# The activation turned by VectorE and through DRAM with a later down projection, and taps' operands of 64 rows for two heads side by side

## The reference

```python
# L0, a long convolution along each sequence, for 32 channels h and 64 batches
mask = (jnp.arange(Lq) < length[:, None]).astype(u.dtype)
u_m = u * mask[:, None, :]
kernel = _get_kernel(log_dt, C, log_A_real, A_imag, Lq)      # 32 x 512 taps
y = irfft(rfft(u_m, 2 * Lq) * rfft(kernel, 2 * Lq))[..., :Lq]
y = (y + u_m * D[:, None]) * mask[:, None, :]
x = x + y
# L1, a gated projection with a low-rank term for each batch
gate = lora_add(x @ W_gate.T, x, A_gate, B_gate)             # 512 -> 1376
up = lora_add(x @ W_up.T, x, A_up, B_up)
act = jax.nn.silu(gate) * up
out = x + lora_add(act @ W_down.T, act, A_down, B_down)      # 1376 -> 512
```

## Time and profile before

| | us |
|---|---|
| median of 3 runs | 544.09 |
| lowest, highest | 543.97, 545.04 |
| profiled execution | 544.7 |
| its span | 543.0 |
| TensorE busy | 505.7 |
| VectorE busy | 344.3 |
| ScalarE busy | 190.5 |
| one tile of the loop | 28.56 |

### The profile page before, as it was taken

How to read it: one execution, slowest core, us unless ns; L and a number is a source line. 1 busy time by engine, 2 the same in 40 slices (tenths; PEclk the granted TensorE clock), 3 DMA queues, 4 the chain that set the end, 5 groups by cost and what they waited for, 6 DMA issues and landing times.

```text
span 543.0 us, 10229 instructions
## 1 busy us (share of the span) xinstructions
PE 505.7 (93%) x3045; PEld 459.8 (85%) x3045; DVE 344.3 (63%) x812; ACT 190.5 (35%) x411; POOL 41.5 (8%) x55
## 2 busy tenths in 40 slices
PE   0098889999999999999999999999999999999997
PEld 0097787989898999989898989898989898999986
DVE  7883266757483939383848475766758483939381
ACT  6790007433333333232324232333333333324220
POOL 1006700101000000000000001000001000001000
PEclk9999899999999999999999999999999999999999
DMA  7899993424132323232323323131414132424200
GB/s 278 277 365 388 320 332 68 111 56 111 46 111 48 114 52 114 52 108 57 96 64 95 66 80 82 53 96 49 114 49 109 43 110 52 114 52 114 53 19 21
DMA packets 68403, 61.59 MB, mean 113 GB/s; under 512 B 41634, under 2 KB 50242, under 8 KB 68386
## 3 DMA queue, kind: packets, MB, share of 16 engines
q1 hardware_dynamic: 68386, 61.39, 39.4%
HBM read 52.89 MB, written 8.47 MB: 113 GB/s over the span
## 4 chain that ended last, share of the span: by engine, by line
PE 86%; DVE 6%; DMA 5%; ACT 1%; issue 1%; SPq 0%; DVEq 0%
PE ps_g L1024 21%; PE ps_u L1024 21%; PE ps_db L1062 13%; PE ps_da L1062 13%; PE ps_x L1004 3%; PE ps_g L978 3%; DMA toep<-kpad 2%; PE ps_x L1053 2%; DMA kpad<-k_sb 2%; PE ps_u L978 2%; PE ps_u L1035 2%; PE ps_u L1034 2%; PE ps_g L1034 2%; PE ps_g L1035 2%; PE ps_da L1123 1%
## 5 line engine op out<-in xcount | busy, mean ns | idle before, releaser
L494 ACT CAST b_spl<-b_raw 64x512 fp32r<-64x512 f32 (+1 forms) x96 | 54.7, 572 | 97.1 <-PE ps_u L1035 78.1
L870 DVE STREAM_TRANSPOSE ps_x<-h_act 32x128 f32<-32x128 f32 x240 | 77.4, 323 | 3.8
L1024 PE MATMUL ps_g<-w_hi,x_hi 128*128 128x512 f32 (+1 forms) x192 | 71.2, 371 | 1.4 <-DVE x_lo L935 1.4
L1024 PE MATMUL ps_u<-w_hi,x_lo 128*128 128x512 f32 (+1 forms) x192 | 71.5, 372 | 0.0
L1024 PE MATMUL ps_u<-w_hi,x_hi 128*128 128x512 f32 (+1 forms) x192 | 71.4, 372 | 0.0
L1024 PE MATMUL ps_u<-w_lo,x_hi 128*128 128x512 f32 (+1 forms) x192 | 71.3, 372 | 0.0
L1024 PE MATMUL ps_g<-w_hi,x_lo 128*128 128x512 f32 (+1 forms) x192 | 71.3, 371 | 0.0
L1024 PE MATMUL ps_g<-w_lo,x_hi 128*128 128x512 f32 (+1 forms) x192 | 71.2, 371 | 0.0
L822 DVE TENSOR_TENSOR b_spl<-b_raw,b_spl 64x512 fp32r<-64x512 f32 (+1 forms) x96 | 63.5, 662 | 4.4 <-ACT b_spl L494 0.7
L1062 PE MATMUL ps_da<-wd_hi,ht_hi 128*128 128x288 f32 (+1 forms) x176 | 54.6, 310 | 0.2 <-DVE ht_lo L879 0.2
L1062 PE MATMUL ps_db<-wd_hi,ht_hi 128*128 128x288 f32 (+1 forms) x176 | 53.1, 302 | 0.0
(11 more groups left out here) (166 smaller groups left out, 939.2 us busy)
## 6 DMA issues: line engine op xcount, KB each, us to landing
a_raw<-atab SPq DMA_DIRECT2D x64, 152.0 KB, 2.3
toep<-kpad SPq DMA_DIRECT2D x16, 512.0 KB, 7.4
b_raw<-btab SPq DMA_DIRECT2D x128, 64.0 KB, 2.1
um<-xr SPq DMA_DIRECT2D x16, 256.0 KB, 5.6
x<-xT SPq DMA_DIRECT2D x8, 512.0 KB, 6.6
w_raw<-wgu SPq DMA_DIRECT2D x8, 512.0 KB, 9.2
xrow<-x_sq SPq DMA_DIRECT2D x64, 64.0 KB, 2.2
y_sb<-xrow SPq DMA_DIRECT2D x16, 256.0 KB, 2.7
```

Source lines behind the costliest of these rows:

```text
L494: nc.scalar.copy(b_spl[0:LR, up, 0:w], b_raw[slot][:, up * w:(up + 1) * w]).then_inc(b_hi, 1)
L870: ins = V.transpose(into[:, :, tok * Q:(tok + 1) * Q], src[:, :, to * Q:(to + 1) * Q])
L1024: T.matmul(ps[:, 0:w], xs[:, kb, :], ws[:, kb, col:col + w], start=(kb == 0 and xs is x_hi and ws is w_hi), stop=False)
```

## The change

Two edits go together.

**Taps of 64 rows.** `toep` has 64 rows for each head of the pair, head 0 on partitions 0 to 63 and head 1 on 64 to 127, each with 576 taps; two DMAs load it. Since a block of 128 input positions is now two halves of 64, `conv` issues for each distance d and each half one matmul of 64 rows for head 0 and one for head 1, which write to the two banks of one PSUM pair. There are three such pairs (`ps_gg`, `ps_uu`, `ps_xx`, the last being the two banks `ps_x`). The host lays out `xr` accordingly.

**Turned activation.** In tiles 1 to 14 all three chunks, in tile 0 chunks 1 and 2, and in tile 15 chunk 0 go through DRAM: VectorE transposes squares of 32 x 32 into `h_sq` (chunks 0 and 2) or `x_sq` (chunk 1) (`square_h`), `store_h` writes them in four DMAs to `hrow`, `load_h` reads the turned rows to one of two buffers `h_raw`, and ScalarE and VectorE split them from there. The other chunks of tile 0 and tile 15 are turned by TensorE. The down projection of chunks 1 and 2 (`down_rest`) moves to the next tile's time, behind its chunk 0; `transpose_td`, `down_lora` and `finish` move behind it. `h_act` has one buffer instead of two. On the A and B rows: `b_raw` is one tensor whose two slots lie on different partitions, and `load_bd` and `load_b` change places.

The diff, cut to its core:

```diff
+RP = 3
+HR = P // 2
+HW = NL + HR
...
+        hrow = nc.dram_tensor("hrow", (FB * P, P), F32, kind="Internal")
...
-            toep = sb(pa, "toep", [P, RC, 2, NL])
+            toep = sb(pa, "toep", [P, RC, HW])
...
-        h_act = sb(top, "h_act", [P, 2, 512])
+        h_act = sb(top, "h_act", [P, 512])
...
+        h_sq = sb(top, "h_sq", [P, 512])
...
+        h_raw = [sb(top, f"h_raw{i}", [P, 4, P]) for i in range(2)]
...
-        ps_g = [top.enter_context(nc.psum_tensor(f"ps_g{i}", [P, 512], F32)) for i in range(2)]
-        ps_u = [top.enter_context(nc.psum_tensor(f"ps_u{i}", [P, 512], F32)) for i in range(2)]
+        ps_c = [top.enter_context(nc.psum_tensor(name, [P, 2, 512], F32)) for name in ("ps_gg", "ps_uu", "ps_xx")]
+        ps_g, ps_u, ps_x = ([both[:, i, :] for i in range(2)] for both in ps_c)
...
+        def shifted_taps(pair, h):
+
+            return bass.AP(tensor=kpad, offset=(2 * pair + h) * (P + NL) + 1, ap=[[1, HR], [1, HW]])
...
-                sp.dma_start(toep[:, slot, :, :], shifted_taps(pair)).then_inc(toep_in[slot], 16)
+                for h in range(2):
+                    sp.dma_start(toep[h * HR:(h + 1) * HR, slot, :], shifted_taps(pair, h)).then_inc(toep_in[slot], 16)
...
+            def store_h(t, c):
+                col, w = CH[c]
+                sp.wait_ge(hsq_ok, NC * t + c)
+                for part in range(P // Q):
+                    rows = x_sq if c == 1 else h_sq
+                    src = rows[part * Q:(part + 1) * Q, 0:w].rearrange("q (f t) -> q f t", t=Q)
+                    into = bass.AP(tensor=hrow, offset=col * P + part * Q, ap=[[P, Q], [Q * P, w // Q], [1, Q]])
+                    sp.dma_start(into, src).then_inc(h_out, 16)
+
+            def load_h(t, c):
+                f0, nf = BLK[c]
+                full = nf if c < NC - 1 else nf - 1
+                sp.wait_ge(h_out, 16 * (P // Q) * (NC * t + c))
+                src = bass.AP(tensor=hrow, offset=f0 * P * P, ap=[[P, P], [P * P, full], [1, P]])
+                sp.dma_start(h_raw[c % 2][:, 0:full, :], src).then_inc(h_in[c], 16)
+                if full < nf:
+                    sp.dma_start(h_raw[c % 2][0:FLAST, full, :],
+                                 hrow.ap()[(f0 + full) * P:(f0 + full) * P + FLAST, :]).then_inc(h_in[c], 16)
...
+                if not first:
+                    store_h(t, 0)
+                if not last:
                     load_b(na, nq, 0, ids)
+                if not first:
+                    load_h(t, 0)
+                if not last:
+                    load_a(na, nq, ids)
+                    store_h(t, 1)
                 if not first:
                     store(*((a, 0) if q == 1 else (a - 1, 1)))
                 if not last:
-                    load_a(na, nq, ids)
+                    load_h(t, 1)
+                    store_h(t, 2)
+                    load_b(na, nq, 1, ids)
+                    load_h(t, 2)
+                    store_x(t + 1)
                     load_bd(na, nq, ids)
-                    load_b(na, nq, 1, ids)
-                    store_x(t + 1)
                     load_y(t + 1, nq)
...
+                def square_h(c):
+                    n = NC * t + c
+                    dve.wait_ge(act_ok, n + 1)
+                    if c == 1:
+                        dve.wait_ge(xrow_out, 16 * (P // Q) * (t + 1))
+                    else:
+                        wait(dve, h_out, 16 * (P // Q) * (n - 1 - c // 2))
+                        wait(dve, htlo_ok, (NC + 1) * t + c // 2)
+                    V.transpose((x_sq if c == 1 else h_sq)[:, 0:CH[c][1]], h_act[:, 0:CH[c][1]]).then_inc(hsq_ok, 1)
...
+                wait(pe, x1_ok, pair - RP + 1)
+                if pair == RP - 1:
+                    pe.wait_ge(amaskt_ok, 1)
+                for d in range(KB):
+                    for half in range(2):
+                        at = d * P + (1 - half) * HR
+                        for h in range(2):
+                            rows = slice(h * HR, (h + 1) * HR)
+                            v = um[rows, slot, half * KB * NB:half * KB * NB + (KB - d) * NB]
+                            last = T.matmul(ps_c[pair % RP][:, h, d * NB:KB * NB], toep[rows, slot, at:at + P], v,
+                                            start=(d == 0 and half == 0), stop=(d == KB - 1 and half == 1))
                 last.then_inc(conv_ps, 1)
...
-                wait(pe, htlo_ok, (NC + 1) * (t - 1) + 1)
+                wait(pe, tm_ok, t)
...
+            def down_rest(t):
+                pe.wait_ge(htlo_ok, (NC + 1) * t + 2)
+                down_chunk(1)
+                pe.wait_ge(htlo_ok, (NC + 1) * (t + 1))
+                for f in range(BLK[2][0], FB):
+                    ins = down(f, 1)
+                ins.then_inc(ad_ps, 1)
+                for f in range(BLK[2][0], FB):
+                    ins = down(f, 0)
+                ins.then_inc(down_ps, 1)
...
                 base(0, 0)
-                if not first:
-                    transpose_td(t - 1)
                 if first:
                     lora_a(t)
-                    base(0, 1)
-                    lora(0, 0)
-                else:
-                    lora(0, 0)
-                    base(0, 1)
+                base(0, 1)
+                lora(0, 0)
                 lora(0, 1)
                 if not first:
-                    down_lora(t - 1)
-                for up in range(2):
-                    base(1, up)
-                    lora(1, up)
+                    down_rest(t - 1)
+                base(1, 0)
                 if first:
                     transpose_act(0)
-                for up in range(2):
-                    base(2, up)
-                    lora(2, up)
-                transpose_act(1)
-
-                pe.wait_ge(htlo_ok, (NC + 1) * t + 1)
+                else:
+                    transpose_td(t - 1)
+                lora(1, 0)
+                base(1, 1)
+                lora(1, 1)
+                if not first:
+                    down_lora(t - 1)
+                base(2, 0)
+                if last:
+                    transpose_act(1)
+                lora(2, 0)
+                base(2, 1)
+                lora(2, 1)
                 wait(pe, y_ok, 2 * t)
                 if first:
                     pe.wait_ge(w_rem_dve, len(pieces) - NP_POOL)
                 pe.wait_ge(ad_lo, t + 1)
+                pe.wait_ge(htlo_ok, (NC + 1) * t + 1)
                 down_chunk(0)
-                transpose_act(2)
-                pe.wait_ge(htlo_ok, (NC + 1) * t + 2)
-                down_chunk(1)
-                if not last:
+                if last:
+                    transpose_act(2)
+                    down_rest(t)
+                else:
                     lora_a(t + 1)
```

More of the change, by code:

```diff
@@ L178, in program @@
         g_ps, u_ps, silu_ok, act_ok = sem("g_ps"), sem("u_ps"), sem("silu_ok"), sem("act_ok")
[L179 removed]
+        hsq_ok, h_out, ht_ps, hthi_ok, htlo_ok = (sem("hsq_ok"), sem("h_out"), sem("ht_ps"), sem("hthi_ok"),
+                                                  sem("htlo_ok"))
+        h_in = [sem(f"h_in{c}") for c in range(NC)]
         ad_ps = sem("ad_ps")
@@ L886, in body @@
+                gated(0)
+                if not first:
+                    square_h(0)
+                b_lo_part(a, q, 1, 0)
+                b_lo_part(a, q, 1, 1)
+                if not first:
+                    td_m_part(t - 1)
                 dve.wait_ge(ad_hi, t + 1)
@@ L890, in body @@
                 if first:
-                    rem_part(NP_GU)
-                    rem_part(NP_GU + 1)
-                b_lo_part(a, q, 1, 0)
-                gated(0)
-                b_lo_part(a, q, 1, 1)
-                if not first:
-                    transpose_first((0, 1))
+                    for n in range(NP_GU, NP_GU + 3):
+                        rem_part(n)
+                    ht_lo_part(t, 0, True)
+                else:
+                    td_lo_part(t - 1)
+                b_lo_part(a, q, 2, 0)
+                gated(1)
+                if not last:
+                    square_h(1)
+                b_lo_part(a, q, 2, 1)
                 if not first:
                     finish(t - 1, 1 - q)
+                    ht_lo_part(t, 0)
                 dve.wait_ge(bd_hi, t + 1)
@@ L970, in conv @@
                 slot = pair % RC
-                pe.wait_ge(toep_in[slot], 16 * (pair // RC) + 16)
+                pe.wait_ge(toep_in[slot], 32 * (pair // RC) + 32)
                 pe.wait_ge(um_in[slot], 16 * (pair // RC) + 16)
-                wait(pe, x1_ok, pair - RC + 1)
-                for h in range(2):
-                    at = h * KB * NB
-                    for d in range(KB):
-                        v = um[:, slot, h * KB * NB:h * KB * NB + (KB - d) * NB]
-                        last = T.matmul(ps_c[slot][:, at + d * NB:at + KB * NB], toep[:, slot, h, d * P:(d + 1) * P],
-                                        v, start=(d == 0), stop=(d == KB - 1))
```

(29 more changed lines are left out.)

214 lines of the change are left out of this document (89 added, 125 removed).

## The result

The changed kernel takes 565.24 us (median of 4 runs, 564.62 to 565.92), the kernel before, on the same chip, 544.5 us (4 runs, 543.97 to 545.04): 1.0377 times as long, interval 1.0357 to 1.0397. The forecast was 558 us, slower.

The account below looks back on a forecast made before the run. TensorE bounds the tiles before, SP's issuing queue after, at 30.0 us a tile. Span 543.0 + 20.2 (tiles 1 to 14) - 0.8 (tile 0) - 6 (convolution) = 556.4, plus 1.7: 558 us, range 548 to 568, chance 0.46.

Parts of the forecast that it names:

- SP's sum: SP's queue per tile: 19.5 + 5.4 + 2.0 + 2.1 + 1.0 = 30.0 us, setting the tile's length.
- break-even: Tile loop: SP's work of 29.0 us a tile, under which the changed kernel would be faster.
- Late first on TensorE: Ahead of `down_chunk(0)`, `htlo` of chunk 0 comes late first; TensorE stands about 2 us a tile there.
- rival 4: Tile loop: idle time lowers TensorE's clock, 0 to 1.4 us a tile, up to 578 us; chance 0.08.
- rival 1: Tile loop: SP keeps up with issues at 0.35, needing 26.7 us; TensorE sets the tile, 528 us; chance 0.22.
- The TensorE term: Tile on TensorE: without the transposes of chunks 1 and 2, 28.56 - 0.77 = 27.79 us.
- Rivals 2 and 3: Convolution matmuls: weight loads in turn, 574 us, chance 0.15; or halves one after another, 596 us, chance 0.09.
- The convolution: Convolution stage: `toep` falls from 512 KB to 288 KB a pair, heads run side by side, gain 6 us.
- A gain of 6 of the 7.6: Convolution stage: TensorE takes back 6 us of 7.6 us lost to waits, the slow pair and the first landing.
- The range: Whole kernel: 548 to 568 us, from SP at 29.1 to 30.6 us a tile and convolution gain 3 to 7.6.

Follow-up runs that it names:

- the run with one read: Changed kernel with the four table indices of a tile read once instead of twice on SP: 539.39 us, 0.9898 of the kernel before.
- the one-stride run: Changed kernel with a pair's 128 tap rows loaded by one DMA, source rows one element apart throughout (second head gets wrong taps): 559.01 us, 1.0257.

## Why the forecast was right in sign and 7 us short

**SP's sum: right, with errors that cancel.** 30.0 us a tile were forecast, 30.0 measured; that they meet to the tenth is luck. Inside it, per tile (SP's records from tile 1 to 15): the new stores took 5.8 us, not 7.4 (a 16-by-32-piece issue takes some 0.49, the row of `store_x` with as many pieces had 0.62; it was taken for the same shape, but the rows of the change have 128x4x32 for the one and 32x16x32 for the other); the loads 1.6, not 2.1 (0.39 for 512 pieces, nearer to the lower bound). Against that stand 1.0 us of short gaps between more records, 0.3 of other records that got longer, 0.1 of register work, 0.5 more waiting than forecast (1.5 instead of 1.0), and 0.2 by which SP's work before was more than the 19.5. It went to the break-even's bad side by 1.0 us, and the run with one read (minus 2.5) to its good side: both sides of the 29.0 are shown.

**Late first on TensorE: right.** `ht_lo` of chunk 0 ahead of the down projection, 16.3 us in 11 waits. I had it at some 2 us a tile; recorded are 1.2 in the mean of 14. A part of the rest is the clock: in one tile the granted clock stayed 1.00 behind such a wait, in another it was 0.65 for the next 4.5 us, part of it at the lower level:

```profile
313.87:318.00 4.13, 4.13 (x33) 4.13 (x33) 3.28 (x6) 1.66 (x3) 1.18 (x2) 1.00 0.73 173
...
373.50:378.00 4.50, 4.47 (x23) 4.47 (x24) 3.19 (x6) 1.66 (x3) 1.17 (x2) 0.65 0.69 167
```

TensorE's busy time is 505.6 us here and 495.2 in the run with one read, for the same 3196 records; 7.2 of these 10.4 us lie in tiles 1 to 14. Part of them is rival 4's mechanism: twice in these tiles, around 257 and 377 us, the granted clock is at its lower level (0.50 of the full one), which it never is there in the run with one read, and each of the two tiles has 29.85 us of busy time where its neighbours have 27.9 to 28.4. It came inside SP's pace and not on top of it. The rest of the 7.2 us are some tenths in each tile with a wait, and no run explains them. The tiles came out 17.3 us longer, forecast 19.4 (20.2 less 0.8): SP has a lead from tile 0 that TensorE uses up first, and the splits of the down weights cost tile 0 2.4 us that only rival 1 had counted.

**The TensorE term: right.** 27.79 forecast, 27.81 measured where SP is out of the way. Rival 1's faster kernel exists, but it needs lighter index reads; by its own condition (issues of many pieces at 0.35) it was wrong: they take 0.39 to 0.50. Rivals 2 and 3 are ruled out by the 2.41 us a pair.

**The convolution: the step that failed.** "A gain of 6 of the 7.6" was a loss of 3.9, which is 9.9 us, more than the whole error of 7 (by the means of the table, a loss of 2.5, it is 8.5). The tiles' 17.3 instead of 19.4 took 2.1 of it back: 9.9 - 2.1 = 7.8 us of span, 564.2 against 556.4. The step was "288 KB, 3.6 MB in all, which at the 311 GB/s of rows 9 is 11.5 us of DMA": it kept the rate and changed the bytes. The rate belonged to transfers over 128 partitions. Between 52 and 62 us the DMA engines were as busy as before (1.06 both) and moved 249 GB/s instead of 330 (before, then after; the last two numbers):

```profile
52.00:62.00 10.00, 6.94 (x39) 6.33 (x37) 1.46 (x2) 1.14 (x2) 5.68 (x4) 0.86 1.06 330
...
52.00:62.00 10.00, 6.91 (x64) 6.33 (x64) 1.70 (x3) 0.00 (x0) 1.46 (x2) 0.83 1.06 249
```

I listed bounds for the matmuls of the pair and none for the rate of the new transfer. With the rate kept (the one-stride run) the start of tile 0 is 2.6 us earlier than before, so even then 6 was too much: the first pair still stands 6.6 us for its landing.

**The range.** 548 to 568 is narrower than what its two terms give together: 29.1 us a tile with a gain of 7.6 is 544 us, 30.6 with a gain of 3 is 569.

What stays open: how much of the 3.9 us is the rate, how much the slow pairs at the lower clock that follow the waits, and how much the spread between executions; whether it is the half of the partitions or the smaller transfer that lowers the rate; and whether the old taps beat the new ones once SP is relieved, 537.94 against 539.39, whose intervals overlap.

## What to carry to other kernels

Add up what the issuing queue does in one round of the loop before moving anything through DRAM: with 12 more stores and 4 more loads a tile it was at 30.0 us against TensorE's 27.8, and the same data path was 1% faster than before once 2.5 us of index reads left the queue. A wait counts as spare only if it is not the queue's own round trip. When a transfer's shape changes, its rate can change too: look at the partitions of its destination and at the outermost dimension of its source, not only at its bytes.

## What the runs showed of the hardware

- Issue on SP: 0.32 us for 16 rows, 0.39 for 128 rows of four 512-byte pieces, 0.47 and 0.49 for 11 and 16 by 32 pieces of 128 bytes, 0.59 for 64 rows of 2304 bytes, 0.62 for 4 by 128 pieces of 128 bytes. The number of pieces alone does not order them.
- Reading one index into a register and checking it takes SP 0.6 us, 0.265 of it the load.
- A DMA of 128 rows whose outermost dimension is 2: 6 us for 288 KB, and the queue behind it held as long; with outermost 128 the same bytes need no such hold.
- With the taps loaded to one half of the partitions at a time, packets of 2048 bytes take 131 to 136 ns in the median, 84 to 89 when every load goes to all 128; a second queue for the other half does not help.
- 64-row matmuls of two heads side by side: 32 records in the 2.41 us of 16 records with 128 rows.
